# Value products in pairs, and second FFN products whole, in a transformer block on one core

## The reference

```
norm(x, g, b) = g * x / sqrt(mean(x*x) + 1e-6) + b      g, b: linear in t, one pair per norm
att(n)        = concat_h( softmax(q_h k_h^T / sqrt(8)) v_h ) Wo^T
y   = x + att(norm(x, g1, b1))
z   = y + ( silu(n2 Wg^T) * (n2 Wh^T) ) Wout^T          n2 = norm(y, g2, b2)
out = x + z
```

## Time and profile before

| | |
|---|---|
| median of three runs | 259.01 us |
| profiled execution | 260.13 us |
| its span | 258.3 us |
| mean granted TensorE clock | 0.96 of full |
| TensorE matmuls busy | 233.9 us, 91% |
| VectorE (DVE) busy | 194.0 us, 75% |
| ScalarE (ACT) busy | 156.7 us, 61% |
| GpSimd (POOL) busy | 97.1 us, 38% |

### The profile page before, as it was taken

One profiled execution on the slowest core, in us unless ns is written; L12 is line 12 of the kernel. 1 busy time (PEld: TensorE's weight loads), 2 busy tenths in 40 slices (PEclk: granted clock), 3 DMA queues, 4 the chain that ended last, 5 costly groups with the idle time before them and its releaser, 6 DMA issues.

```text
span 258.3 us, 8211 instructions
## 1 busy us (share of the span) xinstructions
PE 233.9 (91%) x3096; PEld 194.1 (75%) x3096; DVE 194.0 (75%) x473; ACT 156.7 (61%) x336; POOL 97.1 (38%) x169
## 2 busy tenths in 40 slices
PE   2679678789989999999999999999999999999895
PEld 2468566557767878787878787878787878687894
DVE  4639645655898898889888998889888888655673
ACT  5456645654866686669766776666556655655430
POOL 8653941425224262427242523252323232323320
PEclk9999759965999999999999999999999999999999
DMA  6863304200230024001500060006000000000001
GB/s 162 341 249 125 124 8 177 74 3 4 102 146 5 23 104 148 25 23 56 193 25 25 17 233 25 11 19 244 24 5 25 1 27 22 6 0 23 22 24 41
DMA packets 11203, 18.79 MB, mean 73 GB/s; under 512 B 1468, under 2 KB 4220, under 8 KB 11036
## 3 DMA queue, kind: packets, MB, share of 16 engines
q1 hardware_dynamic: 10780, 17.67, 19.0%
q10 hardware_dynamic: 384, 0.59, 0.6%
HBM read 3.22 MB, written 2.10 MB: 21 GB/s over the span
## 4 chain that ended last, share of the span: by engine, by line
PE 51%; issue 25%; POOL 10%; ACT 5%; DVE 5%; DMA 2%; SPq 0%; POOLq 0%; DVEq 0%; ACTq 0%
PE score L434 9%; PE pv L501 8%; PE proj L565 6%; PE aux L344 4%; PE aux L346 3%; PE aux L345 3%; POOL inv L985 3%; POOL xn_lo L998 2%; POOL xs L991 2%; ACT p_s L683 2%; PE aux L518 2%; DVE nmax L824 2%; DMA qs<-qp 2%; PE aux L522 2%; PE raw L414 1%
## 5 line engine op out<-in xcount | busy, mean ns | idle before, releaser
L683 ACT ACTIVATE p_s<-score 128x1024 f32<-128x1024 f32 x64 | 65.6, 1025 | 38.2 <-PE score L434 38.1
L824 DVE TENSOR_REDUCE nmax<-raw 128x8 f32<-128x1024 f32 x60 | 73.2, 1219 | 11.9 <-PE raw L414 9.0
L434 PE MATMUL score<-qs,ks 32*128 32x128 f32 x512 | 44.0, 290 | 5.0 <-ACT xn L657 2.4
L434 PEld LDWEIGHTS score<-qs,ks 32*128 32x128 f32 x512 | 35.3, 192 | 17.5 <-issue 14.3
L414 PE MATMUL raw<-ks,qs 31*128 31x128 f32 x480 | 41.4, 291 | 1.8 <-DMA qs<-qp 1.8
L501 PE MATMUL pv<-p_s,va 128*32 128x128 f32 x1024 | 42.5, 285 | 0.2 <-ACT xn L701 0.2
L883 DVE SCALAR_TENSOR_TENSOR gated<-th,aux 128x256 f32<-128x256 f32 x56 | 23.3, 415 | 18.6 <-ACT th L712 18.3
L344 PE MATMUL aux<-xn_hi,ffn_hi 128*128 128x256 f32 x112 | 36.5, 326 | 0.0
L998 POOL TENSOR_TENSOR xn_lo<-xn,xn_hi 128x128 fp32r<-128x128 f32 x32 | 14.6, 458 | 58.0 <-DVE xn_hi L874 58.0
L414 PEld LDWEIGHTS raw<-ks,qs 31*128 31x128 f32 x480 | 32.8, 193 | 2.4 <-DMA qs<-qp 2.0
L985 POOL TENSOR_TENSOR inv<-ms,mhalf 128x1 f32<-128x1 f32 x32 | 17.2, 539 | 40.1 <-DVE ms L866 40.1
(11 more groups left out here) (125 smaller groups left out, 430.3 us busy)
## 6 DMA issues: line engine op xcount, KB each, us to landing
ks<-kp SPq DMA_DIRECT2D x23, 256.0 KB, 2.8
qs<-qp SPq DMA_DIRECT2D x23, 256.0 KB, 2.5
out_y<-x_s SPq DMA_DIRECT2D x16, 128.0 KB, 1.8
x_s<-in_x SPq DMA_DIRECT2D x1, 1536.0 KB, 11.4
x_s<-in_x SPq DMA_DIRECT2D x2, 256.0 KB, 3.7
ffn_in_s<-in_ffn_in_w SPq DMA_DIRECT2D x1, 512.0 KB, 6.7
qs<-shift SPq DMA_DIRECT2D x30, 8.0 KB
attn_w_s<-in_attn_w SPq DMA_DIRECT2D x1, 256.0 KB, 5.9
```

The source lines that it names most:

```text
L434: return pe.matmul(score[:, pair_cols(e, j)], ks[buf(g)][tile_rows(e, t, TROWS), j, batch_cols(t)], qs[buf(g)][tile_rows(e, t, TROWS), j, ...
L683: act.activation(p_s[:, n % PBUF, :], score[:], ACT.Exp, scale=SCALE).then_inc(s_exp, 1)
L824: dve.tensor_reduce(heads[:, t % 2, :, :], raw_dst(g, t)[:].rearrange("l (e j m) -> l e j m", e=HALVES, j=HQ), AX.X, ALU.max, negate=True) ...
```

## The change

The value products move by one beat (PV = 2) and are issued in even beats, both tiles of a batch one behind the other; odd beats have none. The output product of half a group is issued whole, in beats 15 and 21 (WSTEP 6, from 5), and its final addition stands in beats 16 and 22. In the first group, the raw product of beat 1 and 2 stands before the value products; the transpose of the second half of the first maxima stands at the end of beat 2; the zero fill of `va[1]` stands before the loop on ScalarE, and GpSimd's `surround_values(1)` before two memsets. The unread products are three in beat 1 and four in each of the beats 2 to 9, ahead of the transpose of `o_s`. The order on VectorE and the order of the other TensorE stages are as they were.

```diff
-    PV = 1
+    PV = 2
-    FFN, OUT, FINAL, WSTEP = 10, 15, 17, HC + 1
+    FFN, OUT, FINAL, WSTEP = 10, 15, 16, HC + 2
...
-                for f, i in due(T - 1, XT2, NB, 2):
+                for f, i in due(T - 2, XT2, NB, 2):
                     pe.wait_ge(s_xn2, NB * f + i + 1)
-                if T == 1:
+                if g == 0 and t == 0:
                     pe.wait_ge(s_shift0, MB)
...
-                for g, t in due(T, PV, BEATS):
-                    c_pv(g, t, T)
                 if 0 < T < APART:
                     for g, t in due(T, RAW, BEATS):
                         b_raw(g, t)
+                for g, i in due(T, PV, NB, 2):
+                    c_pv(g, 2 * i, T)
+                    c_pv(g, 2 * i + 1, T)
+                if T == 1:
+                    pe.wait_ge(s_qlo, 2)
+                    unread_products(proj, 3)
+                elif 1 < T < FFN:
+                    pe.wait_ge(s_max, BEATS - 1)
+                    unread_products(ffn, 4)
                 for g, i in due(T, TRO, NB, 2):
                     c_tro(g, i)
...
-                    for g, half in due(T, OUT + WSTEP * w, 2):
-                        d_out(g, w, half)
+                    for g, _ in due(T, OUT + WSTEP * w):
+                        d_out(g, w, 0)
+                        d_out(g, w, 1)
...
                 for g, half in due(T, MAXT, 2, HQ):
-                    b_maxT(g, half)
+                    if g > 0:
+                        b_maxT(g, half)
...
-                if T == 2 or T == 3:
-                    pe.wait_ge(s_max, BEATS - 1)
-                    unread_products(ffn, 8 if T == 2 else 4)
+                if T == MAXT + HQ:
+                    b_maxT(0, 1)
...
             a_mean(2)
+            zero_fill(va[1][:].rearrange("l b v -> l (b v)"), s_va0[1])
             a_high(1, s_k, key_dst(1), kp, s_khi)
...
-                if T == 1:
-                    zero_fill(va[1][:].rearrange("l b v -> l (b v)"), s_va0[1])
...
             a_scale(3)
+            surround_values(1)
             zero_queries(2)
             zero_keys(2)
-            surround_values(1)
```

## The result

The changed kernel takes 269.73 us (median of four runs, 269.70 to 271.08) against 258.65 us before: 1.041 times as long, 95% interval 1.037 to 1.046. Predicted were 268.4 us, range 260 to 280. Its profiled execution is 269.71 us, with a span of 267.9. Ratios in this document are made from each kernel's fast runs; the profiled executions of e2 and e4 were slower ones, with more low clock in the first beats.

What follows compares the result with a forecast made beforehand. It took TensorE's own work plus its few waits to bound the main part. From the profiled 260.13 us, -1.8 (first group), -2.8 (fillers) and +14.0 (stalls) gave 269.5; the median, 1.1 lower, gave 268.4 us, range 260 to 280.

Steps and rivals of the forecast that it cites:

- The late transpose: Odd beats: transpose of o_s runs no sooner than 4.41 us after the even beat's score, a stall of 0.83 us.
- class 4/5: Beat pairs with T mod 8 of 4 and 5: 7.50 to 7.6 us, today 6.66; +0.95 in each of 6.
- class 6/7: Beat pairs with T mod 8 of 6 and 7: 7.50 us, today 6.42; +1.08 in each of 7.
- class 0/1: Beat pairs with T mod 8 of 0 and 1, no output product: 6.61 us, today 6.66; -0.3 in all.
- class 2/3: Beat pairs with T mod 8 of 2 and 3, key product covering the norm: +0.1 us each, +0.6 in all.
- The bound behind it: Odd beats' gate product needs the previous hidden product: 0.2 us of wait even behind a transpose that waited for nothing.
- The tail: Last beats: at beat 65 the transpose already waits 0.68 us and its gate product starts 0.38 later, +0.4 us.
- The head: First ten beats: -1.8 us from the first group's order and -2.8 us from the fillers.
- The order: First group's rearranged work: beat 2's score -1.06 us, then -0.7 to beat 3's score; sum -1.8, bounds 0 and -3.
- The fillers: Unread products in beats 1 to 9, 35 instead of 12, to hold the clock: -2.8 us, gain between 0 and 4.6.
- The fast one: Rival, odd beats: transpose of o_s not late, at 0.80 us from the score, no stall; 252 us, chance 0.11.
- Half the stall: Rival, main part: 0.35 us a pair in place of 1.0, cancelling the head; 259 to 260 us, chance 0.07.

Runs made afterwards that it cites:

- e2: Changed kernel with single value products again, output products still whole; 261.7 us, 1.009 times the kernel before.
- e4: Changed kernel with the unread products (fillers) of the kernel before; 1.057 times the kernel before.
- e3: Changed kernel with output products in halves again, value products still paired; 259.9 us, 1.001 times the kernel before.
- e5: Changed kernel with the norm that makes o_s ahead of the hidden instructions on VectorE; 265.81 us, 1.023 times the kernel before.
- e9: Changed kernel with eight more unread 128-column matmuls between score and transpose of o_s in odd beats 11 to 63; 273.20 us, 1.051 times the kernel before.
- e1: Changed kernel with single value products and output products in halves again, first beats' order and fillers kept; 256.6 us, 0.987 times the kernel before.
- e6: Changed kernel with gate and up products ahead of the transpose of o_s, ScalarE's copy behind tanh; 267.31 us, 1.031 times the kernel before.
- e7: e3 with gate and up products ahead of the transpose of o_s, ScalarE's copy behind tanh; 1.011 times the kernel before.
- e8: Changed kernel with the whole output product ahead of the transpose of o_s; 267.57 us, 1.033 times the kernel before.
- e11: The same kernel as e1, measured again in more rounds; 255.80 us over six runs, 0.985 times the kernel before.

## Why the prediction was right

**The late transpose.** Right, and by the step that was worked. The transpose was to run 4.41 us after the even beat's score and ran at 4.46, the missing 0.05 being the pair of value products, 1.01 us (92.38, its first row, to 93.39) and not 0.95. Predicted pair lengths were 7.6, 7.5 and 6.61; measured 7.55, 7.63 and 6.65. Against before (same beats in both profiles) class 4/5 lost 5.25 us over six pairs (5.7 predicted), class 6/7 6.7 over the six of the main part (6.5), class 0/1 nothing (-0.3), class 2/3 1.2 (0.6), and beats 12 and 13 0.4 that I had at nothing (e3 has these 0.4 too, so they come with the pairs; why is not shown). That makes 13.6, where the prediction's terms give 12.5 for the main part. e5 and e9 show that it is a wait and for what, e1 to e3 that it comes from the two moves, and that each alone costs 5 to 6 us. Two slips in the working change nothing: there are six pairs of class 0/1 and seven of class 2/3, not seven and six (0.15 us), and the transpose had no time to spare from 0.45 us sooner on, not 0.57.

**What the prediction did not see.** The bound behind it (the gate product needs the hidden product) is real: it is the longest wait that e5 left. But the prediction names one cover of the value product, and there were more: it also hid the exponential, before the input transpose and before the Wo product. In the changed kernel the longer wait hides these, so the sum came out; in e3, e6 and e7 it did not.

**The tail.** 1.5 us predicted (beats 62 and 63 and the transpose of beat 65), 2.7 measured. From the exponential of beat 62 to the transpose of beat 65, which waited 0.68 us and now waits 1.55, it is 1.8 us more. The longer wait is not the later gate product's, as the prediction has it: e3, with the pairs, still waits 0.68, and e2, with whole output products alone, 1.55. In each of the two this stretch is 0.9 us longer than before (9.73 and 9.71 for 8.82). Another 0.9 comes behind it, which I had not looked for. There the second norm's transpose of the last batch stands 4.5 us after that transpose in both kernels, but it waits 1.04 us for GpSimd's scaled tile where it waited 0.15, and the output half of beat 68 that filled this time before now comes after it:

```profile
250.47 0.33 PE L518 MATMUL aux<-ident,o_s 128*128 128x128 f32 x1 [1.55 <-DVE o_s L858]
...
254.99 0.33 PE L530 MATMUL pv<-ident,xs 128*128 128x128 f32 x1 [1.04 <-POOL xs L998]
```

That the whole output product is the reason is shown by e2 against e1, which differ in it alone. From this transpose of the last batch to the end it is 12.9 us in the changed kernel and in e2, and 11.9 before, in e1 and in e3. e2's transpose there waits 1.04 us as well.

**The head.** -4.6 predicted, -6.7 measured. The order was to give 1.8; e4 leaves 0.5 to 1.2 for the order and the pairs of the first beats together. And the pairs saved time there: the head is 33.57 us in e1 and 32.47 in e3, which has the value products in pairs, with a low stretch of 6.8 us in both. The prediction had put a second value product at the low clock down as 0.9 us more. Beat 2's score did come at 29.51 (29.75 predicted) and beat 3's at 35.73 instead of 39.12, but under a low stretch of 6.8 us in place of 10.3, so that the fillers' part is in it. The fillers were to give 2.8 and gave 4 (times) to 5.5 (profiles). The zero fill cost nothing: ScalarE still waited 0.67 us for the key product behind it. That the total is so near is luck. Against the profile before, the terms were off by -2.1 us in the head, +1.1 in the main part and +1.2 in the tail, and these cancel to 0.2. The step from profile to median took off 1.1 us, which the kernel before had between them and the changed kernel has not (269.71 and 269.73); that is nearly all of what the forecast of 268.4 misses.

**The rivals.** The fast one needed the transpose at 0.80 us from the score; it was at 1.62 in beat 21 and 1.20 in beat 23. Half the stall: no, the pairs have their full length. The clock had one low stretch in the head and not two, and in e4, without the new fillers, it was low again near 57 us. No stall made it fall: the main part was granted 1.00 throughout, with TensorE busy 25.76 of 29.07 us in a group.

## What to carry to other kernels

In an engine that is nearly full, an instruction is also the time that it gives to the others. Before moving one, list every wait behind it that it covers, not only the longest, and look at where the chain starts that it covers: here the cover was taken from the odd beat and the chain was made 0.4 us later in the even one, which added up. A wait can be filled with work that is ready, but that work delays what stands behind it: e8 got 3.3 of 8.6 us in this way, and e6, which changed the order of the neighbours, 0.8 of 7. And first see whether the gain that one is after sits in another part of the same edit, as it did here in the fillers of the first beats.

## What the runs showed of the hardware

The clock in the head differs between executions of the same work. With the fillers, the low stretch (1.2 GHz) was one of 6.8 us in place of two of 10.3, and before it TensorE had been busy 2.16 of 3.00 us (25.0 to 28.0). In the profile of e5, which changes nothing on TensorE, it was one of 3.4 us, and the head took 31.26 us and not 32.46. The kernel e11 was granted 0.966 to 0.987 of full over its runs and took 258.2 to 254.6 us.

Eight float32r matmuls of 128 columns took about 0.9 us, and not the half of what eight with 256 columns take that I had assumed. In e9 they start 0.11 us apart at the full clock; those of 256 columns in the head of the changed kernel start 0.12 apart. Though the weights stay the same, the trace shows a weight load for each of the eight, and these too start 0.11 us apart. That the loads set the pace is likely, but no run tried it.

Twenty-two us of extra work in the waits of the changed kernel cost 3.5 us, and 23 in the full kernel e1 cost 22.9. Work that is put into a wait which another engine sets was mostly free here.
